# A delta-net layer on one core: four idle-bank matrix products per element, and a new written order

## The reference

```
xn = layernorm(x)
q, k, v = silu(conv4(xn @ Wq)), silu(conv4(xn @ Wk)), silu(conv4(xn @ Wv))    # 12 heads, 64/64/128 wide
gk, beta = -exp(A_log) * softplus(xn @ Wgk + dt_bias), sigmoid(xn @ Wb + b_b)
q, k = l2norm(q) * SCALE, l2norm(k)
for each token: S = S * exp(gk); S = S + k outer ((v - k.S) * beta); o = q.S
o = o * rsqrt(mean(o * o) + 1e-5) * g_norm * g * sigmoid(g),   g = xn @ Wg
y = x + o @ Wo + fp4_linear(silu(fp4_linear(xn, w_gate)) * fp4_linear(xn, w_up), w_down)
```

## Time and profile before

| | |
|---|---|
| median of 3 runs | 3064.13 us (3057.14 to 3064.31) |
| the profiled execution | 3054.66 us |
| its span, first to last instruction | 3052.9 us |
| PE busy | 2657.3 us (87%) |
| DVE busy | 2522.1 us (83%) |
| ACT busy | 2201.2 us (72%) |
| POOL busy | 1625.6 us (53%) |
| mean granted TensorE clock | 0.939 of 2.4 GHz |

### The profile page before, as it was taken

The page is one execution under the profiler, slowest core; times in us unless marked ns, Lnnn a source line. Parts: engine busy times, 40 slices in busy tenths (PEclk is TensorE's granted clock), DMA queues, the critical chain, the costliest instruction groups (busy, mean ns, idle before and its releaser), DMA issues.

```text
span 3052.9 us, 83158 instructions
## 1 busy us (share of the span) xinstructions
PE 2657.3 (87%) x25361; PEld 2131.6 (70%) x25487; DVE 2522.1 (83%) x7140; ACT 2201.2 (72%) x6626; POOL 1625.6 (53%) x2418
## 2 busy tenths in 40 slices
...
GB/s 64 22 34 35 15 33 35 35 24 35 16 34 35 24 35 25 24 35 24 35 36 14 35 29 30 36 16 34 36 27 32 35 16 34 35 24 35 33 16 23
DMA packets 319431, 91.35 MB, mean 30 GB/s; under 512 B 283057, under 2 KB 310001, under 8 KB 318961
## 3 DMA queue, kind: packets, MB, share of 16 engines
...
HBM read 46.76 MB, written 38.80 MB: 28 GB/s over the span
## 4 chain that ended last, share of the span: by engine, by line
PE 54%; DVE 25%; issue 11%; ACT 4%; POOL 3%; DMA 1%; DVEq 1%; SPq 0%; ACTq 0%; POOLq 0%
DVE KQ L914 6%; PE ring L1382 5%; PE ring L1228 5%; DVE UP L1010 5%; PE bank_o L1349 4%; PE ring L1211 4%; PE ring L1178 3%; PE ring L1169 3%; PE bank_e L1318 3%; PE bank_e L1331 3%; PE bank_e L1335 2%; PE ring L1241 2%; DVE ssr L979 2%; PE bank_o L1355 2%; PE bank_e L1326 2%
## 5 line engine op out<-in xcount | busy, mean ns | idle before, releaser
L614 POOL TENSOR_TENSOR laneA<-laneA,laneT 96x30 f32<-96x30 f32 (+14 forms) x960 | 520.3, 542 | 75.3
L611 POOL TENSOR_TENSOR laneT<-laneA 96x30 f32<-96x30 f32 (+14 forms) x960 | 498.9, 520 | 68.0
L914 DVE SCALAR_TENSOR_TENSOR KQ<-ring,ckq,KQ 128x255 f32<-128x255 f32 (+2 forms) x1152 | 460.5, 476 | 17.5 <-DVE nabs L949 6.5
L914 DVE SCALAR_TENSOR_TENSOR vc<-ring,cvv,vc 128x255 f32<-128x255 f32 (+2 forms) x1152 | 462.8, 476 | 3.9 <-ACT vc L718 0.8
L598 POOL TENSOR_TENSOR sqk<-sse,phalf 128x8 f32<-128x8 f32 x96 | 157.4, 1639 | 576.9 <-DVE sse L984 576.9
L1010 DVE SCALAR_TENSOR_TENSOR UP<-ring,cj,gm 128x256 f32<-128x256 f32 x768 | 327.2, 478 | 26.7 <-PE ring L1195 14.9
L1055 DVE SCALAR_TENSOR_TENSOR V<-bank_o,negG,V 128x128 f32<-128x128 f32 x384 | 134.3, 350 | 202.9 <-PE bank_o L1355 146.3
L592 POOL TENSOR_TENSOR gm<-g,mle 128x512 f32<-128x512 f32 x192 | 197.6, 1051 | 179.0 <-DVE UP L1010 165.9
L1211 PE MATMUL ring<-xnT,wv 128*128 128x256 f32 x768 | 231.8, 430 | 62.7 <-DVE KQ L914 53.9
L1169 PE MATMUL ring<-gm,mgt 128*128 128x512 f32 x384 | 218.7, 654 | 59.1 <-DVE UP L1010 58.3
L1178 PE MATMUL ring<-xnT,wqk 128*128 128x256 f32 x768 | 237.2, 446 | 36.6 <-issue 34.5
...
...
## 6 DMA issues: line engine op xcount, KB each, us to landing
to_lanes<-UP SPq DMA_DIRECT2D x128, 96.0 KB, 2.7
...
UP<-from_lanes SPq DMA_DIRECT2D x128, 96.0 KB, 3.0
...
```

Source lines behind the costliest of these rows:

```text
L611: link(nc.gpsimd.tensor_tensor(t, A[:, 0:m, j:j + 1].broadcast_to([LANES, m, n]), A[:, j:j + 1, j + 1:BLK].broadcast_to([LANES, m, n]), AL ...
L614: link(nc.gpsimd.tensor_tensor(w, w, t, ALU.add))
L914: ins = nc.vector.scalar_tensor_tensor(acc[:, n, s:T], src[:, n * T:n * T + T - s], wt(n)[:, TAPS - 1 - s:TAPS - s], acc[:, n, s:T], ALU.m ...
```

## The change

A new step `KW` is put into the list four times an iteration. In each, PE multiplies the identity by 512 columns of the value weights and writes the result over the whole of `bank_o`, where nobody reads it: the scan's own first products (slot 5) write over it. It waits only for DVE's last read of `bank_o` in the scan before.

The list itself is a new one. Offsets and steps are the same but for `VPs 4` (now in the iteration that makes its taps) and `XR` (now fetched one iteration ahead, at the end). ACT's copy of `XN` gets a wait for an older product, `GP 5` of two elements before. `KEEP` gets four more pairs.

```
@@ the step itself, in PE's program
+                    if kind == "KW":
+
+                        if not zero(i):
+                            pe.wait_ge(s_or, cnt(i, len(O_SLOTS), 0))
+                        mm(BO[:, :], ident[:, :], wv[:, 0:4 * P], start=True, stop=True)
@@ in ACT's program
                     if kind == "XN":
+                        if not early(i):
+
+                            split(act, full("XN", 0), full("GP", 5))
+                            act.wait_ge(full("GP", 5), rv(i - 2, "GP", 5))
@@ the start of the list, about a quarter of it
-    ("QK", 0, 1), ("VT", 3, 0), ("ZB", 0, 1), ("VPs", 4, 0), ("VTr", 3, 0), ("STORE", 0, 0), ("QK", 1, 1),
-    ("QK", 2, 1), ("QKr", 0, 1), ("VT", 2, 0), ("ZBr", 0, 1), ("VPs", 5, 0), ("ZBe", 0, 1), ("QKt", 0, 1),
-    ("QK", 3, 1), ("ZBg", 0, 1), ("QKr", 1, 1), ("DDg", 0, 1), ("VTr", 2, 0), ("VP", 0, 1), ("VT", 5, 0),
-    ("QKt", 1, 1), ("QKr", 2, 1), ("QKr", 3, 1), ("GC", 0, 1), ("TSTORE", 0, 0), ("VT", 4, 0), ("DDg", 1, 1),
-    ("QKt", 2, 1), ("GCr", 0, 1), ("QKs", 0, 1), ("VP", 1, 1), ("VPr", 0, 1), ("QKs", 1, 1), ("QKt", 3, 1),
-    ("QT", 0, 1), ("QK", 4, 1), ("DDg", 2, 1), ("VTr", 5, 0), ("VTr", 4, 0), ("VPr", 1, 1), ("QTr", 0, 1),
-    ("DDg", 3, 1), ("DD", 0, 1), ("QKs", 2, 1), ("VPt", 1, 1), ("QKs", 3, 1), ("TFETCH", 0, 0), ("VP", 2, 1),
-    ("QKr", 4, 1), ("QT", 1, 1), ("FETCH", 0, 0), ("DDr", 0, 1), ("DD", 1, 1), ("QKt", 4, 1), ("VPr", 2, 1),
-    ("QT", 2, 1), ("QTr", 1, 1), ("QTr", 2, 1), ("DD", 2, 1), ("MY", 0, 0), ("MY", 1, 0), ("QN", 0, 1),
-    ("DDr", 1, 1), ("VPt", 2, 1), ("DDr", 2, 1), ("MY", 2, 0), ("MYr", 0, 0), ("VPt", 0, 1), ("QK", 5, 1),
-    ("MZ", 0, 0), ("QKr", 5, 1), ("QT", 3, 1), ("MZr", 0, 0), ("MYr", 1, 0), ("DD", 3, 1), ("QN", 1, 1),
...
+    ("QK", 0, 1), ("VPs", 5, 0), ("QKr", 0, 1), ("ZB", 0, 1), ("KW", 0, 0), ("ZBr", 0, 1), ("VT", 3, 0),
+    ("ZBe", 0, 1), ("QK", 1, 1), ("VT", 2, 0), ("QKt", 0, 1), ("QK", 2, 1), ("VT", 5, 0), ("ZBg", 0, 1),
+    ("VTr", 3, 0), ("VTr", 2, 0), ("QKr", 1, 1), ("DDg", 0, 1), ("VT", 4, 0), ("GC", 0, 1), ("QKt", 1, 1),
+    ("QKr", 2, 1), ("VTr", 5, 0), ("GCr", 0, 1), ("QKs", 0, 1), ("VP", 0, 1), ("QK", 3, 1), ("QKr", 3, 1),
+    ("QKs", 1, 1), ("QKt", 2, 1), ("VP", 1, 1), ("VTr", 4, 0), ("VPr", 0, 1), ("VPr", 1, 1), ("QT", 0, 1),
+    ("TSTORE", 0, 0), ("VP", 2, 1), ("STORE", 0, 0), ("QTr", 0, 1), ("VPr", 2, 1), ("QKt", 3, 1), ("VPt", 1, 1),
+    ("QK", 4, 1), ("QKs", 2, 1), ("KW", 1, 0), ("QT", 1, 1), ("DDg", 1, 1), ("DD", 0, 1), ("TFETCH", 0, 0),
+    ("QTr", 1, 1), ("QKr", 4, 1), ("QKs", 3, 1), ("KW", 2, 0), ("QT", 2, 1), ("KW", 3, 0), ("DD", 1, 1),
+    ("DDg", 2, 1), ("FETCH", 0, 0), ("QTr", 2, 1), ("DDr", 0, 1), ("DDr", 1, 1), ("QN", 0, 1), ("DD", 2, 1),
+    ("MY", 0, 0), ("VPt", 2, 1), ("MY", 1, 0), ("VPt", 0, 1), ("MY", 2, 0), ("MYr", 0, 0), ("QK", 5, 1),
+    ("QKt", 4, 1), ("MZ", 0, 0), ("DDg", 3, 1), ("QT", 3, 1), ("QN", 1, 1), ("QN", 2, 1), ("DDr", 2, 1),
...
@@ the middle, from the reads of the last key products to the feed-forward
-    ("XQ0", 1, 1), ("MY2r", 1, 0), ("QTr", 5, 1), ("QN", 4, 1), ("DDr", 4, 1), ("GRr", 5, 1), ("QN", 5, 1),
-    ("SE", 4, 0), ("GR", 3, 1), ("GR", 4, 1), ("MZ", 2, 0), ("GRr", 6, 1), ("MZr", 2, 0), ("SO", 5, 0),
-    ("SE", 5, 0), ("DD", 5, 1), ("SSr", 2, 1), ("GRr", 7, 1), ("MX", 2, 0), ("DDr", 5, 1), ("CJ", 2, 1),
-    ("GRr", 8, 1), ("VPs", 0, 1), ("SO", 6, 0), ("GRr", 9, 1), ("MZ2r", 1, 0), ("SE", 6, 0), ("GR", 5, 1),
-    ("GRr", 10, 1), ("SE", 7, 0), ("GRr", 11, 1), ("SO", 7, 0), ("MY2r", 2, 0), ("XQ", 0, 1), ("VP", 3, 1),
...
+    ("QT", 5, 1), ("VPs", 2, 1), ("GRr", 4, 1), ("GRr", 5, 1), ("DD", 4, 1), ("SE", 3, 0), ("QTr", 5, 1),
+    ("MZ", 2, 0), ("DDr", 4, 1), ("MY2r", 1, 0), ("GR", 3, 1), ("QN", 4, 1), ("SE", 4, 0), ("DD", 5, 1),
+    ("XQ0", 0, 1), ("QN", 5, 1), ("GRr", 6, 1), ("GRr", 7, 1), ("MZr", 2, 0), ("SSr", 2, 1), ("SO", 5, 0),
+    ("SE", 5, 0), ("CJ", 2, 1), ("GR", 4, 1), ("GR", 5, 1), ("DDr", 5, 1), ("GRr", 8, 1), ("MX", 2, 0),
+    ("GRr", 9, 1), ("GRr", 10, 1), ("SE", 6, 0), ("GRr", 11, 1), ("SO", 6, 0), ("VP", 3, 1), ("MZ2r", 1, 0),
+    ("XQ0", 1, 1), ("SO", 7, 0), ("SE", 7, 0), ("XQ", 0, 1), ("XQr", 0, 1), ("GP", 0, 0), ("VPr", 3, 1),
+    ("SO", 8, 0), ("SE", 8, 0), ("VPt", 3, 1), ("FU", 0, 1), ("FUr", 0, 1), ("SE", 9, 0), ("SO", 9, 0),
...
@@ the end
-    ("YO", 0, 0), ("OSQ", 0, 0), ("OG", 3, 0), ("GPr", 4, 0), ("WO", 0, 0), ("OT", 2, 0), ("KTr", 1, 1),
-    ("LANEP", 4, 1), ("LANEP", 5, 1), ("GP", 5, 0), ("OT", 3, 0), ("HQ", 3, 1), ("WO", 1, 0), ("VPr", 5, 1),
-    ("GPr", 5, 0), ("OG", 4, 0), ("OTr", 2, 0), ("HT", 0, 1), ("OTr", 3, 0), ("OT", 4, 0), ("VT", 0, 1),
-    ("HTr", 0, 1), ("OG", 5, 0), ("WO", 2, 0), ("XN", 0, 2), ("OT", 5, 0), ("WO", 3, 0), ("VPt", 5, 1),
-    ("HT", 1, 1), ("OTr", 4, 0), ("VT", 1, 1), ("LANEP", 6, 1), ("HTr", 1, 1), ("OTr", 5, 0), ("XNr", 0, 2),
-    ("VTr", 0, 1), ("VTr", 1, 1), ("WO", 4, 0), ("WO", 5, 0), ("LANEP", 7, 1), ("YOr", 0, 0),
+    ("OG", 2, 0), ("KT", 1, 1), ("GP", 4, 0), ("LANEP", 3, 1), ("SO", 17, 0), ("GPr", 3, 0), ("SQ", 17, 0),
+    ("HQ", 1, 1), ("SE", 17, 0), ("VP", 5, 1), ("SQ", 18, 0), ("SE", 18, 0), ("SO", 18, 0), ("OG", 3, 0),
+    ("YO", 0, 0), ("WO", 0, 0), ("OS", 2, 0), ("OT", 2, 0), ("OSQ", 0, 0), ("HQ", 2, 1), ("OTr", 1, 0),
+    ("GP", 5, 0), ("GPr", 4, 0), ("VPs", 3, 1), ("LN2", 0, 2), ("OTr", 2, 0), ("LANEP", 4, 1), ("OT", 3, 0),
+    ("KTr", 1, 1), ("HQ", 3, 1), ("WO", 1, 0), ("OG", 4, 0), ("LANEP", 5, 1), ("VPs", 4, 1), ("VPr", 5, 1),
+    ("WO", 2, 0), ("GPr", 5, 0), ("LANEP", 6, 1), ("HT", 0, 1), ("XN", 0, 2), ("OTr", 3, 0), ("OT", 4, 0),
+    ("LANEP", 7, 1), ("XNr", 0, 2), ("OTr", 4, 0), ("WO", 3, 0), ("VT", 1, 1), ("OG", 5, 0), ("OT", 5, 0),
+    ("WO", 4, 0), ("HT", 1, 1), ("VTr", 1, 1), ("HTr", 0, 1), ("XR", 0, 1), ("VPt", 5, 1), ("OTr", 5, 0),
+    ("HTr", 1, 1), ("WO", 5, 0), ("YOr", 0, 0),
```

More of the change, by code:

```diff
@@ L25 @@
 TURNED = 3
-KEEP = ((("ZBr", 0, 1), ("XQ0", 0, 1)), (("ZB", 0, 1), ("QK", 2, 1)), (("ZBr", 0, 1), ("QKt", 2, 1)), (("QK", 2, 1), ("FU", 0, 1)), (("GPr", 0, 0), ("OG", 0, 0)), (("GPr", 1, 0), ("OG", 1, 0)), (("GPr", 2, 0), ("OG", 2, 0)), (("GPr", 3, 0), ("OG", 3, 0)), (("GPr", 4, 0), ("OG", 4, 0)), (("GPr", 5, 0), ("OG", 5, 0)))
+KEEP = ((("KW", 0, 0), ("SO", 5, 0)), (("KW", 1, 0), ("SO", 5, 0)), (("KW", 2, 0), ("SO", 5, 0)), (("KW", 3, 0), ("SO", 5, 0)), (("ZBr", 0, 1), ("XQ0", 0, 1)), (("ZB", 0, 1), ("QK", 2, 1)), (("ZBr", 0, 1), ("QKt", 2, 1)), (("QK", 2, 1), ("FU", 0, 1)), (("GPr", 0, 0), ("OG", 0, 0)), (("GPr", 1, 0), ("OG", 1, 0)), (("GPr", 2, 0), ("OG", 2, 0)), (("GPr", 3, 0), ("OG", 3, 0)), (("GPr", 4, 0), ("OG", 4, 0)), (("GPr", 5, 0), ("OG", 5, 0)))
 WEIGHTS_AT = ("FU", 0)
@@ L64 @@
-    ("MZ", 0, 0), ("QKr", 5, 1), ("QT", 3, 1), ("MZr", 0, 0), ("MYr", 1, 0), ("DD", 3, 1), ("QN", 1, 1),
-    ("DDr", 3, 1), ("SSr", 0, 1), ("QTr", 3, 1), ("CJ", 0, 1), ("MY2", 0, 0), ("GR", 0, 1), ("QKt", 5, 1),
-    ("GRr", 0, 1), ("GRr", 1, 1), ("QKs", 4, 1), ("MY2r", 0, 0), ("QN", 2, 1), ("MZ", 1, 0), ("QKs", 5, 1),
-    ("MZr", 1, 0), ("GR", 1, 1), ("QN", 3, 1), ("GRr", 2, 1), ("SSr", 1, 1), ("MYr", 2, 0), ("GR", 2, 1),
[10 rows of a table removed]
-    ("GP", 0, 0), ("MZ2r", 2, 0), ("SQ", 11, 0), ("LANEP", 0, 1), ("FUm", 1, 1), ("VPs", 1, 1), ("LANEP", 1, 1),
[12 rows of a table removed]
@@ new lines @@
+    ("DDg", 2, 1), ("FETCH", 0, 0), ("QTr", 2, 1), ("DDr", 0, 1), ("DDr", 1, 1), ("QN", 0, 1), ("DD", 2, 1),
+    ("MY", 0, 0), ("VPt", 2, 1), ("MY", 1, 0), ("VPt", 0, 1), ("MY", 2, 0), ("MYr", 0, 0), ("QK", 5, 1),
+    ("QKt", 4, 1), ("MZ", 0, 0), ("DDg", 3, 1), ("QT", 3, 1), ("QN", 1, 1), ("QN", 2, 1), ("DDr", 2, 1),
+    ("DD", 3, 1), ("QKr", 5, 1), ("MZr", 0, 0), ("QTr", 3, 1), ("DDr", 3, 1), ("SSr", 0, 1), ("MYr", 1, 0),
+    ("MY2", 0, 0), ("QKt", 5, 1), ("GR", 0, 1), ("CJ", 0, 1), ("GRr", 0, 1), ("GRr", 1, 1), ("GR", 1, 1),
@@ new lines @@
+    ("GRr", 2, 1), ("MY2r", 0, 0), ("QKs", 4, 1), ("QN", 3, 1), ("MZ", 1, 0), ("GRr", 3, 1), ("MZr", 1, 0),
+    ("QT", 4, 1), ("VPs", 0, 1), ("DDg", 4, 1), ("GR", 2, 1), ("MX", 1, 0), ("QKs", 5, 1), ("MYr", 2, 0),
+    ("DDg", 5, 1), ("SSr", 1, 1), ("QTr", 4, 1), ("LN", 0, 2), ("CJ", 1, 1), ("MZ2r", 0, 0), ("VPs", 1, 1),
+    ("QT", 5, 1), ("VPs", 2, 1), ("GRr", 4, 1), ("GRr", 5, 1), ("DD", 4, 1), ("SE", 3, 0), ("QTr", 5, 1),
+    ("MZ", 2, 0), ("DDr", 4, 1), ("MY2r", 1, 0), ("GR", 3, 1), ("QN", 4, 1), ("SE", 4, 0), ("DD", 5, 1),
```

1 line of the change is left out of this document (added), and 20 rows, old and new, of the table ORDER.

## The result

The changed kernel takes 3015.05 us (median of 4 runs, 3012.09 to 3022.08) beside 3064.22 for the kernel before (4 runs, 3057.14 to 3066.81): ratio 0.9846, 95% interval 0.9823 to 0.9870, 1.5% faster. The forecast was 3034. The profiled span fell from 3052.9 to 3012.4 us, by 40.5; the sum had said 30.

The account below looks back on a forecast made before the run. An element was taken as about 50 us of DVE work, then 40 of PE work. Plain elements -0.5 us over 31 (-15) and the branch -15 gave 3025 profiled, 3034 as median; range 2975 to 3100, likeliest case 3005 to 3055.

Parts of the forecast that it names:

- seam: Between elements, ZB ahead of VT 3 and VPt 5 behind VTr 1 bring QKt 1 earlier: -0.7 us per element.
- middle: Around GRr and scan: same DVE work before SO 7 (0), GP 0 moved (-0.86), waits for ACT's copies (+0.4 us).
- tail: Behind SO 18, HQ 2 and LN2 stand before OG 4, whose bank XN awaits: +1.2 us per element.
- the elements with the branch: ZB ahead of VT 3 makes ZBg's small instructions mostly miss GpSimd's copy: 2.1 us in seven of twelve, -15 us.
- The products: Four KW products in the DVE half, 3.4 us per element, taken as covered: 0, with ends of 0 and 110 us.
- rival C: Products run at low clock, PE reaches QK 5 late, DVE waits: +1.6 us per element, about 3099 us; chance 0.15.
- The clock: Low stretch at DD 5 partly goes, -0.5 us per element; the opening's shrinks, worth 0 to 0.4 us.
- rival A: Opening at full clock returns most of 3.1 us: -2.5 us per element, -78 in all, to 2986; chance 0.13.
- `GP 0`: GP 0 moves in front of SO 8, out of the half that PE fills: -0.86 us per element.
- the same DVE work: Before SO 7: XQ0 1 (about 2.0 us) moves from before GRr 5 to behind SO 6, at no cost.
- rival D: OG 4 later than thought, inverse eats its slack: +1.5 to 2 us more per element, 3080 to 3095; chance 0.14.
- The inverse: From TFETCH to its use on PE: up to 1 us of some 3 us slack eaten, at no cost.

Follow-up runs that it names:

- 5: Changed kernel with two small DVE instructions of ZBg (eb + 1 and its reciprocal) moved into CJ 0: 3002.17 us, ratio 0.9824 to the kernel before.
- 6: Changed kernel without the four KW products, with the same two small DVE instructions moved into CJ 0: 2983.99 us, ratio 0.9764 to the kernel before.
- 9: Kernel 5 with KW 1 to 3 alone, KW 0 left out: 2983.29 us, ratio 0.9743 to the kernel before.
- 10: Kernel 5 with KW 0 alone, KW 1 to 3 left out: 2984.61 us, ratio 0.9745 to the kernel before.
- 3: Changed kernel with each of the four KW products done twice: 3057.24 us, ratio 0.9998 to the kernel before.
- experiment 1: Changed kernel's order with all four KW products left out: 2997.28 us, ratio 0.9801 to the kernel before.
- experiment 2: Kernel before, order kept, with four KW products added, two before VT 4 and two before VP 1: 3046.60 us, ratio 0.9957 to the kernel before.
- 12: Kernel 6 with GP 0 put back behind MZ2 2, as in the kernel before: 3017.27 us, ratio 0.9856 to the kernel before.
- Experiment 4: Changed kernel with ZB put back behind VT 3 and VPt 5 ahead of VTr 1: 3021.16 us, ratio 0.9887 to the kernel before.
- 8: Kernel 5 with both parts of the quantisation XQ0 put back ahead of GRr 5: 3109.51 us, ratio 1.0167 to the kernel before.
- 7: Kernel before with the two small DVE instructions of ZBg moved into CJ 0: 3036.66 us, ratio 0.9936.
- kernel 11: Kernel 6 with VPt 5 put ahead of VTr 1: 2980.58 us, ratio 0.9738 to the kernel before.

## Why the prediction was right, and where it was not

The direction and the range held; the time came 19 us below the forecast. Behind that stand terms that were right, and four that were off: seam, middle, tail and the elements with the branch. That the sum came so near is in part luck: the seam came 1.3 us per element above its term, the tail 1.4 below.

**The products, taken as 0 (ends 0 and 110).** Their duration was right, 0.86 us each on the chain. With all four the cost is 18 us of 3060 (5 against 6); with one or with three, none that can be measured (9, 10); with eight, `QKt 5` waits for the keys (3): the path of rival C, but only at twice the change's dose, and at a clock of 0.973, so by the work added and not by a low clock. So they are no gain in this order, and all four are a small loss, which the changed kernel carries. Its gain comes from the written order: 2.0% by experiment 1.

**The clock, -0.5 per element at `DD 5`, 0 to 0.4 in the opening; rival A, -78 us.** The term at `DD 5` was right. In the trace before, the stretch from the first `GRr` to the last takes 20.6 us in the eight plain elements without low clock in it, and 21.4 to 21.8 in the six with it; the mean of 21.04 is 0.46 above the former, and in the kernel after no plain element has low clock there. The low stretch of the opening shrank and did not vanish, as expected, but mostly by the order (1). What it is worth, products paid, experiment 2 shows: 0.6 us of a plain element's first half, and 11 us in all for a mean of 0.966 instead of 0.939. That refutes A, which had 2.5 us an element. But DVE's short waits in the earlier trace rows do not make the low clock free: in the kernel after, the four plain elements without a low stretch take 88.9 us, nine with one 89.4 to 89.8, and one with a longer one 90.7. The Trainium skill (TensorE: Matmul & The Clock Gate, Part 1) puts the ramp's penalty under 1% of a typical span. It speaks there of the ramp as a kernel starts, while here the clock fell anew in nearly every element, so the 31 us that the prediction drew from it as a bound on any effect of the clock does not follow. The 0.4% that experiment 2 gained is below that 1% all the same.

**`GP 0`, -0.86.** Right: 0.95 (12). In the new order its move is worth about 30 us; in the old order it was not tried.

**The seam, -0.7.** Wrong. `ZBr` did come 1.25 us sooner, but the first `GRr` comes 0.6 later after `YOr`, not 0.7 sooner. Two moves of DVE's own work, seen in the timelines and not isolated by a run, fill what was won. `VTr 3`'s copy, which stood ahead of `ZBr`, now stands behind `ZBg` and ahead of `QKt 1`, which so begins 6.6 us after `YOr` instead of 6.7, and not at 6.1. And a third `QN` (0.6 us) now stands ahead of the first `GRr` instead of behind it, so that 0.6 of the +1.83 is only moved from the next stretch. The copy, before and after:

```profile
1679.81 0.69 DVE L1001 TENSOR_TENSOR V<-ring,sqk 128x512 f32<-128x512 f32 x1 [0.97 <-PE ring L1219]
```

```profile
1107.25 0.69 DVE L1006 TENSOR_TENSOR V<-ring,sqk 128x512 f32<-128x512 f32 x1 [0.23 <-DVE beta L966]
```

Experiment 4 shows the choice between the two seams to be neutral for a plain element.

**The middle, 0 for "the same DVE work", -0.86 + 0.4 for the rest.** The two stretches around the last `GRr` together changed by -3.52 + 2.10 = -1.42; the forecast for them, with the 0.5 of clock at `DD 5`, was -0.96. The prediction has no term for `cj`, whose 0.84 us fell away there (seen in the traces, in no run by itself). The rest of the -3.52 is mostly work that DVE now does elsewhere: `XQ0 1`, the third `QN`, and some reads of the scan. `XQ0 1` is not five instructions of 2.0 us, as the prediction and the list of steps ahead of it have it, but the last three, 1.27 us; the first seven are `XQ0 0`. And the premise failed as a test (8): with the quantisation ahead of `GRr 5` the new order is 3.75 us longer per element, with the same DVE work before `SO 7`. The premise asked only when DVE has finished its work, not when PE gets its banks: `GR 3` to `5` stand behind that work, and their reads by DVE behind them. PE stands 3.5 us at `GR` when it is placed so, about as long as the quantisation takes. The wait at `SO 7`, put at 2 us, is 0.7.

```profile
1148.35 0.71 PE L1354 MATMUL bank_o<-Sb,KQ 128*128 128x128 f32 x4 [0.75 <-DVE qse L1062]
```

**The tail, +1.2.** Wrong in sign: the stretch from `SO 18` to `YOr` went from 11.70 to 11.47. `XN` waits at most 0.2 us, not 1.2. This is the largest term that was off, 1.4 us per element, 44 us in all if it had been alone; it was the base of rival D, which fell with it.

**The inverse, 0.** Right. In the plain element shown `TFETCH` is issued at 1117.17 and its use begins at 1121.93, with no wait on PE:

```profile
1117.17 1.45 SPq L529 DMA_DIRECT2D N<-turned_lanes  x3
```

```profile
1121.93 1.72 PE L1264 MATMUL ring<-N,UP 32*32 32x32 f32 x96
```

4.8 us from issue to use instead of 6.9: the slack went down by two, not by the one expected at most, and was unpaid.

**The elements with the branch, -15.** Half right. The nine that are not blocked take 92.63 on average instead of 95.66 for the eleven before; had all twelve been so, they would have given 36 us. But the step "the small instructions mostly miss the copy" holds only for the first, `sp` (0.18 us). The third, `eb`, now begins with the copy, in three elements, and pays 4.8 to 5.05 us. Beyond the plain element's gain the twelve gave 12 x (1.54 - 1.06) = 6 us. The order moved the collision from one instruction to the next; experiments 5 to 7 take it away.

**The sum.** Per plain element -0.5 was forecast and -1.06 came: seam -0.7 forecast, +0.58 came; middle with the clock at `DD 5` -0.96, -1.42 came; tail +1.2, -0.23 came. Times 31 that is 33 us instead of 15 (the first three elements gained more, 2.4 each). With the branch's 6 instead of 15, it makes 39 of the 40.5.

What stays open: what sets PE's wait at the branch, and with it a part of the products' cost. It is 36 to 38 us in all, up to 4.3 to 4.5 at once, in the changed kernel and experiments 4 and 5, and 42.7 in experiment 2; but experiment 8 has all four products too and 31.3, experiment 3 has eight and 33.2, about as without any (31.6 to 32.8). So the number of products alone does not decide it. Open is also why the first three elements gained 2.4 us each, and how much of the gain is `cj`'s. All of this was only seen. The combinations that were not run: kernel 11 with any product, and `GP 0` moved in the old order alone.
